# The last conditioning stage of a four-layer kernel written as one program of two halves of tiles, with the dispatch and both routers rewritten

## The reference, cut to what matters

```python
ada = t_emb @ w_ada + b_ada                      # 32 x 1536: six rows of 256 for each sequence
sh_msa, sc_msa, g_msa, sh_mlp, sc_mlp, g_mlp = jnp.split(ada, 6, axis=-1)
xn = layer_norm(logmap0(x))
xm = expmap0(xn * (1 + sc_msa) + sh_msa)
q, k, v = (_to_heads(plin(xm, w, b)) for w, b in qkv)        # 16 heads of 16, 256 -> 3 x 256
out_h = expmap0(softmax(logmap0(q) @ logmap0(k).T / 4) @ logmap0(v))   # inside one sequence of 64
attn_out = plin(_from_heads(out_h), w_o, b_o)                # 256 -> 256
x = mobius_add(x, expmap0(g_msa * logmap0(attn_out)))
xn = layer_norm(logmap0(x))
xm = expmap0(xn * (1 + sc_mlp) + sh_mlp)
ff = plin(plin(xm, w_f1, b_f1), w_f2, b_f2)                  # 256 -> 1024 -> 256
return mobius_add(x, expmap0(g_mlp * logmap0(ff)))
```

## Time and profile before

| | before |
|---|---|
| time, median of 3 | 2611.76 us |
| time of the profiled execution | 2609.6 us |
| its span, first to last instruction | 2607.9 us |
| mean granted TensorE clock | 0.862 of 2.4 GHz |
| TensorE busy | 2185.6 us (84%) |
| VectorE busy | 1433.2 us (55%) |
| ScalarE busy | 932.7 us (36%) |
| GpSimd busy | 224.3 us (9%) |

### The profile page before, as it was taken

How to read it: one execution, slowest core, us unless ns; L and a number is a source line. 1 busy time by engine, 2 the same in 40 slices (tenths; PEclk the granted TensorE clock), 3 DMA queues, 4 the chain that set the end, 5 groups by cost and what they waited for, 6 DMA issues and landing times. The chain is left out here.

```text
span 2607.9 us, 34388 instructions
## 1 busy us (share of the span) xinstructions
PE 2185.6 (84%) x13525; PEld 1763.6 (68%) x13525; DVE 1433.2 (55%) x2771; ACT 932.7 (36%) x1755; POOL 224.3 (9%) x172
## 2 busy tenths in 40 slices
PE   6688699999799999999998846899575975985786
PEld 5477578888687888888887744699443853474554
DVE  2789555777575444444432144666257357516785
ACT  2133255555244444444442202245122232322322
POOL 0044200000000000000000000288200000000000
PEclk7599799999799999999999955799867565986998
DMA  1274312222013111111000002453300000000000
GB/s 50 97 234 134 74 51 65 97 97 98 1 40 91 33 35 47 33 33 34 15 1 9 4 1 82 155 142 76 75 18 1 2 7 9 16 19 34 1 8 25
DMA packets 102739, 133.24 MB, mean 51 GB/s; under 512 B 6132, under 2 KB 90035, under 8 KB 102324
## 3 DMA queue, kind: packets, MB, share of 16 engines
q1 hardware_dynamic: 92468, 117.21, 14.1%
q0 software_dynamic: 10112, 13.85, 3.1%
HBM read 109.25 MB, written 21.79 MB: 50 GB/s over the span
## 5 line engine op out<-in xcount | busy, mean ns | idle before, releaser
L1563 DVE TENSOR_TENSOR m_h_lo<-m_hf,m_h_hi 128x512 fp32r<-128x512 f32 x256 | 172.1, 690 | 360.8 <-ACT m_hf L1538 358.9
L1535 ACT ACTIVATE m_h_hi<-m_h_ps,m_bT 128x512 fp32r<-128x512 f32 x256 | 177.0, 691 | 369.5 <-PE m_h_ps L394 349.9
L1538 ACT ACTIVATE m_hf<-m_h_ps,m_bT 128x512 f32<-128x512 f32 x256 | 175.0, 684 | 0.0
L594 POOL DMA_INDIRECT token_sums<-e_y,slot_row x56 | 145.3, 2595 | 160.2 <-DVE e_y L697 148.0
L659 ACT ACTIVATE e_h_hi<-e_h_ps,e_b1T 128x320 fp32r<-128x320 f32 (+1 forms) x128 | 77.9, 609 | 170.5 <-PE e_h_ps L394 165.3
L1275 DVE TENSOR_TENSOR c_h_lo<-c_hf,c_h_hi 128x512 fp32r<-128x512 f32 x120 | 82.3, 687 | 74.3 <-ACT c_hf L1234 73.1
L2051 PE MATMUL f_o_ps<-f_w,f_srcT 128*128 128x256 f32 (+1 forms) x384 | 119.4, 463 | 0.0
L713 DVE TENSOR_TENSOR e_h_lo<-e_hf,e_h_hi 128x320 fp32r<-128x320 f32 (+1 forms) x128 | 74.2, 590 | 79.6 <-ACT e_hf L662 78.1
L394 PE MATMUL m_y_ps<-m_h_hi,l_w_1hi 128*128 128x512 f32 x256 | 100.9, 394 | 3.4 <-issue 3.4
L394 PE MATMUL m_h_ps<-m_x_hi,l_w_0hi 128*128 128x512 f32 x256 | 101.1, 395 | 0.4 <-ACT m_b2T L1528 0.4
L1231 ACT ACTIVATE c_h_hi<-c_h_ps,c_b 128x512 fp32r<-128x512 f32 x88 | 61.7, 701 | 109.9 <-PE c_h_ps L394 109.3
(11 more groups left out here) (658 smaller groups left out, 5626.4 us busy)
## 6 DMA issues: line engine op xcount, KB each, us to landing
cT<-in_L_ffn_W_dram SPq DMA_DIRECT2D x30, 1024.0 KB, 5.6
res<-in_L_cond_ew_dram SPq DMA_DIRECT2D x22, 1024.0 KB, 5.1
cT<-in_L_ffn_w_dram SPq DMA_DIRECT2D x16, 1024.0 KB, 6.2
res<-gates_rows SPq DMA_DIRECT2D x8, 1024.0 KB, 9.4
token_rows<-d_tok SPq DMA_DIRECT2D x2, 2112.0 KB, 7.8
token_sums<-res SPq DMA_DIRECT2D x2, 2048.0 KB, 7.6
res<-token_sums SPq DMA_DIRECT2D x2, 2048.0 KB, 8.3
res<-in_x_dram SPq DMA_DIRECT2D x1, 2048.0 KB, 8.3
```

The source lines that it names most:

```text
L594: pool.indirect_dma_start(out=sums, out_offset=bass.IndirectOffsetOnAxis(ap=st.slot_row[0:r, e, j:j + 1], axis=0), in_=y[0:r, e % 2, j, :] ...
L1535: act.activation(hs[0][:, f, :], h_ps[:, f % HB, :], ACT.Relu, bias=bT[:, at:at + 1])
L1538: act.activation(hf[:, f % HB, :], h_ps[:, f % HB, :], ACT.Relu, bias=bT[:, at:at + 1]).then_inc(act_done, 1)
L1563: dve.tensor_tensor(hs[1][:, f, :], hf[:, f % HB, :], hs[0][:, f, :].bitcast(F32), ALU.subtract).then_inc(h_ready, 1)
```

## The change

1. **Modulation** (new class). `ada` is now computed in `l0_router_phase`, some 1800 us earlier, and stored to DRAM (`modulation_rows`, 32 × 1536). TensorE's products stand between the router's logits and its prefix sum; ScalarE copies the result; SyncE stores it and waits for the store. `sel` is gone. In layer 3, SyncE loads the rows spread over the 64 partitions of their sequence, four tiles at a time, in two buffers for shift and scale and two for the gates, as the norms and gates free them.
2. **One program for layer 3 conditioning.** The eleven phases become one block. A generator, `l3_order`, lists stages of single tiles, and each engine writes its part of each stage in that order. Tiles 0 to 7 and 8 to 15 are one step apart: the norm of the second half runs in the projections of the first, the projections of tiles 10 to 15 in the attention of the first, the output projection, gate and sum of the first half in the attention of the second, those of the second half in w_f1 and w_f2 of the first, and so on. All weights are loaded ahead. PSUM is one tensor of 8 banks: 4 for scores, 1 for turned q and k, 1 for attention's output, which leaves 1 for a turned tile and 1 for its product while both are under way.
3. **Work moved between engines.** Sums of squares are taken by ScalarE with the square (`accum_out`) for norms, w_o, w_f1 and w_f2; the dot product is one VectorE instruction with `accum_out` instead of two; attention's output is copied and squared on ScalarE, and its division by the sum is folded into the later scaling; `x * a1` of the gate's end moves to ScalarE; the scaling of v is folded into its copy.
4. **Dispatch**: `hot` is made by 8 `tensor_tensor` instructions of 128 × 2048 (float16 operands) instead of 128 of 128 × 128; `grouped` by 12 contiguous instructions; TensorE has `hot` as the moving operand and 16 columns of `grouped` as weights; the result is copied by ScalarE and turned by TensorE.
5. **Layer 2 router**: scores are turned once so that a partition holds one expert and tile; a step compares them with four candidates by four `tensor_scalar` with `accum_out`, of 128 × 128.

The core of the order:

```diff
+    for t in range(HALF):
+        b = t + HALF + 2
+        yield from attend(t, HALF)          # head_scale t+3, score t+1
+        if b < NT:
+            yield from narrow(b, (0,))      # qkv_turn b, a third of its product
+        yield from attend_turn(t, HALF)     # attn_turn t+2
+        if b < NT:
+            yield from narrow(b, (1,))
+        yield from attend_out(t, 0)         # weigh t, head_sum t-1
+        if b <= NT:
+            yield "qkv_sum", b - 1
+        if b < NT:
+            yield from narrow(b, (2,))
...
+    for t in range(HALF, NT):
+        i = t - HALF
+        yield from attend(t, NT)
+        if i == 0:
+            for n in range(HALF):
+                yield "attn_scale", n
+            yield "attn_clip", 0
+            yield from project(range(0, 2))
+        if i == 1:
+            yield from project(range(2, 5))
+        if i == 2:
+            yield from project(range(5, 8))
+            yield "gate_len", 0
+        if i == 3:
+            yield from gated(0)
+        if i == 4:
+            yield "tanh", 0
+        if i == 5:
+            yield from moved(range(0, HALF))
...
+        yield from attend_turn(t, NT)
+        if i == 4:
+            yield "gate_fac", 0
...
+        yield from attend_out(t, HALF)
...
+    for t in range(HALF):
+        if 2 <= t + 1 < HALF:
+            yield "f1_turn", t + 1
+        yield "f1", (t, 0)
+        yield "f1", (t, 1)
...
+        if 2 <= t < 6:
+            yield from project(range(HALF + 2 * (t - 2), HALF + 2 * (t - 1)))
+        if t == 6:
+            yield "gate_len", 1
+        if t == 7:
+            yield from gated(HALF)
+    yield "f1_len", 0
+    yield "tanh", 1
+    yield "f2_turn", (0, 0)
```

The load of the modulation, the norm that reads it, and the dispatch's core:

```diff
+            def rows(out, c, at, sem_in):
+                for a in range(2):
+                    first = (c % 4) * CHUNK
+                    width = out.shape[2]
+                    src = ada_rows.rearrange("(t a) n -> a t n", a=2)[a, first:first + CHUNK, at:at + width]
+                    sp.dma_start(out[a * S:(a + 1) * S, :, :], src.partition_broadcast(S)).then_inc(sem_in, 16)
...
+                dve.scalar_tensor_tensor(out=xn[:, m % 2, :], in0=(x if m < NT else dst)[:, t, :], scalar=mv[:, t, 0:1],
+                                         in1=mod[:, k % 2, m % CHUNK, D:2 * D], op0=ALU.subtract, op1=ALU.mult).then_inc(normed, 1)
...
+                dve.scalar_tensor_tensor(out=v[:, t, :], in0=xn[:, m % 2, :], scalar=s[:, t:t + 1],
+                                         in1=mod[:, k % 2, m % CHUNK, 0:D], op0=ALU.mult, op1=ALU.add).then_inc(v_done, 1)
```

```diff
-            for n in range(E8 * NT):
-                if n >= HOTS:
-                    dve.wait_ge(hot_used, n - HOTS + 1)
-                dve.tensor_scalar(hot[:, n % HOTS, :], places[:, :], place[:, n // NT, n % NT:n % NT + 1], None,
-                                  ALU.is_equal).then_inc(hot_made, 1)
+            for e in range(2, E8):
+                dve.tensor_tensor(hot[:, e, :, :], places[:, :, :], bc(place[:, e, :], 1, P), ALU.is_equal).then_inc(hot_made, 1)
```

And a step of the layer 2 router:

```diff
-                then(dve.tensor_tensor(reached[:, :, :, :], bc(sc[:, :, :], 1, WAYS), bc(cand[:, :, :], 3, NT), ALU.is_ge))
-                dve.tensor_reduce(part[:, :, :], reached[:, :, :, :], AX.X, ALU.add).then_inc(counted, 1)
+                for w in range(WAYS - 1):
+                    dve.tensor_scalar(reached[:, w, :], scT[:, :], cand[:, w:w + 1], 0.0, ALU.is_ge, ALU.add,
+                                      accum_out=part[:, w:w + 1]).then_inc(step_done, 1)
+                    n[0] += 1
```

More of the change, by code:

```diff
@@ L852, in _ @@
             r.load(sp, W, b)
+            ada.load(sp, w_ada, b_ada)
+            ada.store(sp, ada_rows)
         @block.gpsimd
@@ new lines, in modulation, with gate, weight @@
+            def modulation(c):
+                if c >= 2:
+                    sp.wait_ge(v_done, CHUNK * (c - 1))
+                rows(mod[:, c % 2, :, :], c, SH_MSA if c < 4 else SH_MLP, mod_in[c % 2])
+            def gate(c):
+                if c >= 2:
+                    sp.wait_ge(z_done, CHUNK * (c - 1))
+                rows(gates[:, c % 2, :, :], c, G_MSA if c < 4 else G_MLP, gate_in[c % 2])
+            def weight(out, W, sem_in):
+                sp.dma_start(out, W.rearrange("(c p) n -> p c n", p=P)).then_inc(sem_in, 16)
@@ L2160, in _ @@
+            gate(0)
+            gate(1)
+            weight(w_f1[:, :, :], w["w_f1"], f1_in)
+            bias(b_f1[:, :], w["b_f1"], f1_in)
+            weight(w_f2[:, :, :], w["w_f2"], f2_in)
+            bias(b_f2[:, :], w["b_f2"], f2_in)
+            modulation(4)
+            modulation(5)
+            gate(2)
+            gate(3)
+            modulation(6)
+            modulation(7)
+            for c_ in range(4, 8):
+                gate(c_)
         @block.gpsimd
@@ L2215, in _, with norm_len @@
+            stages = dict(qkv_turn=qkv_turn, qkv=qkv_part, attn_turn=attn_turn, score=score, weigh=weigh, wo_turn=wo_turn, wo=wo,
+                          f1_turn=f1_turn, f1=f1, f2_turn=f2_turn, f2=f2)
+            for stage, i in l3_order():
+                if stage in stages:
+                    stages[stage](i)
         @block.scalar
         def _(act):
-            def keep(t):
-                act.wait_ge(turned, t + 1)
+            square = Squares()
+            def norm_len(h):
+                act.wait_ge(n2_done, h + 1)
+                act.activation(half(n, h), half(n2x, h), ACT.Sqrt).then_inc(n_rooted, 1)
@@ new lines, in tanh, with move @@
+            def tanh(h):
+                act.wait_ge(squared, square.of["gate", HALF * (h + 1) - 1])
+                act.activation(half(nz, h), half(n2z, h), ACT.Sqrt).then_inc(nz_rooted, 1)
+                act.wait_ge(thin, h + 1)
+                act.activation(half(th, h), half(nz, h), ACT.Tanh).then_inc(tanhed, 1)
+            def move(m):
+                act.wait_ge(weights_done, m // HALF + 1)
+                if m >= 2:
+                    act.wait_ge(moved, m - 1)
+                t = m % NT
+                act.activation(part[:, m % 2, :], (x if m < NT else dst)[:, t, :], ACT.Copy, scale=a1[:, t:t + 1]).then_inc(parted, 1)
@@ L2446 @@
+            for stage, i in l3_order():
+                if stage in stages:
+                    stages[stage](i)
+            dve.wait_ge(moved, 2 * NT)
 QB = 16
```

1317 lines of the change are left out of this document (800 added, 517 removed).

## The result

The changed kernel takes 2501.51 us (median of 4 runs, 2497.92 to 2503.27) against 2611.73 (2609.91 to 2611.98): a ratio of 0.9578, 95% interval 0.9561 to 0.9594, so 110 us less. The forecast was 2509, range 2440 to 2555. The profiled execution has a span of 2500.2 us, 107.7 under the old one.

The account below looks back on a forecast made before the run. Layer 3's stages each have their own bound while other engines mostly idle, and attention runs at 1.2 GHz. −87 − 18 + 1.5 + 1 = −102.5 from 2609.6 gives 2507, as median 2509; own range 2485 to 2535, whole 2440 to 2555.

Parts of the forecast that it names:

- The stage, 442 forecast: Layer 3 conditioning, walked in the new order: 442 us against 529.4, 87 less.
- The terms: Norm 49, heads 21, attention 72, between 12, attention 82, w_f1 60, wait 12, w_f2 39+2, w_f1 37, w_f2 37, gate 19.
- the second (+6): Layer 3: head factors, two narrow tiles and first scalings, 21 us, with 1.5 us a narrow third.
- the sixth (+4): Layer 3: norm and w_f1 of 8 tiles with 8 w_o tiles, 60 us.
- The clock: TensorE's granted clock in layer 3: mixed in the attentions, 0.9 or more in w_f1 and w_f2.
- Rival B: TensorE stays at 1.2 GHz in both layer 3 attentions: 2546 us; chance 0.15.
- Rival A: Layer 3: charged queue waits run through, both attentions reach 2.4 GHz: stage 385, total 2452 us; chance 0.28.
- Rival D: Layer 3: the order does not overlap, only removed work and dispatch count: 2534 us; chance 0.07.
- C: Slower than before: TensorE at 1.2 GHz also in projections, w_f1 and w_f2: 2703 us; chance 0.05.
- Dispatch, 9 each: Both dispatches: place to `slot_row` 21 instead of 30.5 us, 9 saved each, between 5 and 13.
- Layer 0 router, +1.5: Modulation added there: 0.5 us for TensorE's products, 1 us for copy, store and landing.
- Layer 2 router, +1: 15 steps between 7 less and 6 more, taken as 0, plus 1 us for two turns.

Follow-up runs that it names:

- experiment 3: Second half's gates, tanh, moves moved into w_f2's steps, against the changed kernel: 2500.37 us; chain pulled together, plus GpSimd's dispatch fills made by ScalarE: 2496.71 us.
- experiment 2: Side work taken out of both attention loops and put behind them, same instructions, against the changed kernel: 2558.23 us, stage 499.5 us.
- Experiment 1: Changed kernel with the old dispatch and old layer 2 router, modulation and new layer 3 stage kept: 2523.32 us.
- packed: Changed kernel with ScalarE making GpSimd's dispatch fills and one-hots grouped by 2 tiles (first dispatch) or 4 (second): 2501.49 us.
- layouts: Changed kernel with ScalarE making GpSimd's dispatch fills, 128 places adjacent in the first dispatch, `grouped`'s 32 columns adjacent in the second: 2503.8 us.

## Why the prediction was right, point by point

- *The stage, 442 forecast.* 444.65 in the changed kernel and 439.8 to 444.3 in the eight others whose stage is untouched. These fall into two groups, by when the clock rises in the first attention: from 77 to 101 us into the stage it is 0.78 to 0.82 in the six at 439.8 to 441.9, and 0.57 to 0.59 in the three at 443.7 to 444.65. The terms, forecast and measured: 49 and 50; 21 and 27; 72 and 69; 12 and 12; 82 and 81; 60 and 64; 12 and 10; 39 + 2 and w_f1's 37 together 78, measured 74; 37 and 38.5; 19 and 19. The worst is the second (+6): the clock was 0.50 there, so a narrow third took 2.7 us instead of 1.5. The next is the sixth (+4). The sum is nearer than its terms, whose errors cancel in part.
- *The clock.* Mixed, as forecast, in the first attention, where I took 72 between 61 and 93: 69 were measured, with the clock rising within the loop, as assumed. In the second it was luck: I took the middle of 75 at the fast clock and 90 at the slow one. The clock was for the most part the slow one (0.54), so my own steps gave 90, and 81 were measured. The three steps with w_o took 14.2, 14.7 and 15.3 for 15, 15 and 16, but the tanh step 6.5 for 10.5 and the last two together 9.8 for 13. My prices for the other engines' work in these steps were too high. Rival B's clock was there in the second attention, its price was not.
- *Rival A (queues couple less)* fails: the gap before w_f2 exists, 9.7 us for 12, and experiment 3 shows that it moves and does not vanish. *Rival D* fails by experiment 2, *C* by 0.95 and 0.96 in w_f1 and w_f2 (second half; 0.85 and 0.96 in the first). The products there were not unchanged, as I wrote: 5.0 and 3.9 us more, as some of them run at the low clock after a wait.
- *The range.* The forecast's own 2485 to 2535 is narrower than the bounds it is said to come from, which add up to 2483 and 2546. Nothing hangs on it.
- *Dispatch, 9 each.* 9.6, by errors that cancel. From place to `slot_row` it was 18.9 us for the 21 forecast: one-hots 1.2 as forecast, TensorE's products 12.5 for 14, `grouped` 2.2 for 3, copy and factors as charged. The stall of 3 us on GpSimd's fills, before that, was not in the sum.
- *Table loads.* 24 in the stage for 26, 1.28 us each as in the earlier trace rows.
- *Layer 0 router, +1.5, measured +3.5.* The term that was missized is TensorE's 0.5 us: with the clock at 0.50 the products outlast the 9.69 us gap of the earlier trace rows by 2.8. The store's 1 us was right: VectorE is done at 78.17 and the block ends at 79.77. Experiment 1 has the 0.5 in an execution where the clock rose earlier.
- *Layer 2 router, +1, measured -3.7.* A step went from 3.18 to 2.83 us: a comparison with its sum starts every 0.27 us, nearer the lower end of my bounds.
- *The rest,* -3.7 in unchanged code from layer 0's experts to layer 2: it follows the dispatch (1384.1 and 1384.3 with the old one, 1379.3 to 1381.7 in the twelve kernels with a new one), and 2.7 of it arise between the last store of the rounded weights (278.1, now 273.5) and layer 1's first load (321.8, now 314.5). How, is open.

## What to carry over

Price an engine's stretch at both clocks, and read the granted clock again after a change of order: here the order of the same instructions moved it from 0.50 to 0.88 in most of one loop and only to 0.54 in the other. Before moving a chain out of a gap, ask between which two points it must lie; if both stay, the gap moves along. An operand's layout has a price on every engine that touches it, on the one that fills it too.

## What the runs showed of the hardware that I had not expected

- A float32 `tensor_scalar` of 128x128 in SBUF lasted 3.24 us beside GpSimd's fills and 0.23 without them; `scalar_tensor_tensor` 0.29 beside them. Beside GpSimd's iota it lasted 8.96 and 2.02 us, each time to the iota's end (packed). The 16-bit one-hots never ran beside a fill, so that case is open.
- 128 streamed bf16 columns cost TensorE 98 ns when they are 16 values apart, at either clock; 65 at 4 apart and 2.4 GHz; at 2 or 1 apart 36 at 2.4 GHz and 60 at 1.2.
- GpSimd's iota of 128x2048 took 1.90 us with an innermost dimension of 128, 2.46 with 16, 4.47 with 4 and 11.37 with 2.
- VectorE's instructions that write 128x128 bf16 values lasted 0.22 to 0.28 us with the values adjacent and 0.51 to 1.03 with them 32 apart (layouts).
- VectorE's 16-bit comparison of 2048 elements took 1.18 to 1.22 us with 2, 4 or 16 adjacent values of both operands innermost, and 2.28 with one value repeated (they start 1.14 and 2.2 us apart).
- The clock stayed at 0.50 through 46.5 us of attention with TensorE busy for 42.4 of them (experiment 2).
